# Node and attention rows gathered into the FFN by edge place, and a new order of its products on TensorE

## The reference, cut to what matters

```python
x = _layernorm(x + L0(x, rel_embed, norm, src, dst, rel_id, ...))     # x1
...
att = agg.reshape(n, NH * HD) @ Wo + bo        # agg is zero where the node has no incoming edge
x = residual + att                             # x2
h = _layer_norm(x, g2, b2)
ffn = gelu(h @ W1 + bf1, approximate=False) @ W2 + bf2
...
x = _layernorm(x1 + (x2 + ffn))
```

## Time and profile before

| | |
|---|---|
| median of 3 runs | 2438.21 us (2438.11 to 2440.93) |
| the profiled execution | 2436.44 us |
| its span, first to last instruction | 2434.7 us |
| mean granted TensorE clock | 0.962 |
| PE busy | 2066.7 us, 85% |
| DVE busy | 1912.1 us, 79% |
| ACT busy | 1330.5 us, 55% |
| POOL busy | 1228.3 us, 50% |
| DMA packets and volume | 353686, 413.33 MB |

### The profile page before, as it was taken

How to read it: one execution, slowest core, us unless ns; L and a number is a source line. 1 busy time by engine, 2 the same in 40 slices (tenths; PEclk the granted TensorE clock), 3 DMA queues, 4 the chain that set the end, 5 groups by cost and what they waited for, 6 DMA issues and landing times. The chain is left out here.

```text
span 2434.7 us, 49516 instructions
## 1 busy us (share of the span) xinstructions
PE 2066.7 (85%) x14383; PEld 1685.0 (69%) x14383; DVE 1912.1 (79%) x7786; ACT 1330.5 (55%) x3176; POOL 1228.3 (50%) x1418
## 2 busy tenths in 40 slices
PE   3777777759997888849999399992999999999998
PEld 2555555559997888737776289881777777777776
DVE  3999999978885889869997877773777777777774
ACT  1899999933332455568886200001556666566665
POOL 2764444247772777667772157775333333333332
PEclk9999999989998999979999699996999999999999
DMA  3888888779997688655552156664133333333321
GB/s 85 259 259 242 243 244 241 212 216 292 295 287 242 197 231 237 185 153 164 162 161 75 48 144 195 202 200 152 54 110 111 105 105 105 109 110 108 105 96 53
DMA packets 353686, 413.33 MB, mean 170 GB/s; under 512 B 51340, under 2 KB 235040, under 8 KB 353418
## 3 DMA queue, kind: packets, MB, share of 16 engines
q1 hardware_dynamic: 315850, 339.88, 44.3%
q0 software_dynamic: 34496, 69.37, 11.4%
q10 hardware_dynamic: 3072, 0.92, 0.2%
HBM read 263.50 MB, written 179.89 MB: 182 GB/s over the span
## 5 line engine op out<-in xcount | busy, mean ns | idle before, releaser
L1807 PEld LDWEIGHTS p_y<-w,g_T 128*128 128x128 f32 x3136 | 365.4, 192 | 46.4 <-issue 24.2
L1807 PE MATMUL p_y<-w,g_T 128*128 128x128 f32 x3136 | 365.8, 275 | 0.0
L1825 ACT ACTIVATE nT<-p_n 128x512 f32<-128x512 f32 x98 | 58.5, 597 | 560.3 <-PE p_n L1815 560.3
L1800 PE MATMUL p_f<-nT,w 128*128 128x512 f32 x784 | 354.0, 594 | 0.0
L1790 POOL TENSOR_TENSOR rstd<-var,minus_half 128x4 f32<-128x4 f32 x98 | 113.8, 1161 | 450.3 <-ACT res L1838 450.1
L547 POOL DMA_INDIRECT x_dst<-in_x_dram,idx x196 | 192.2, 981 | 226.9 <-DMA edge_x<-x_dst 144.3
L1832 ACT ACTIVATE g_T<-p_f,bf 128x512 f32<-128x512 f32 x392 | 266.7, 680 | 31.1 <-PE p_f L1800 31.0
L901 POOL DMA_INDIRECT h_src<-h_table,idx x196 | 189.5, 967 | 104.1 <-issue 58.6
L1800 PEld LDWEIGHTS p_f<-nT,w 128*128 128x128 f32 x784 | 141.9, 191 | 141.4 <-issue 141.4
L1597 POOL DMA_INDIRECT x_rows<-xv,idx x196 | 195.6, 998 | 77.8 <-issue 55.2
L1130 POOL DMA_INDIRECT x_src<-x_rows,idx x196 | 184.9, 943 | 85.4 <-issue 55.5
(11 more groups left out here) (321 smaller groups left out, 5548.6 us busy)
## 6 DMA issues: line engine op xcount, KB each, us to landing
xs<-x_rows SPq DMA_DIRECT2D x98, 512.0 KB, 3.7
x_in<-in_x_dram SPq DMA_DIRECT2D x98, 256.0 KB, 4.1
h_table<-h_rows SPq DMA_DIRECT2D x98, 256.0 KB
x_rows<-x_in SPq DMA_DIRECT2D x98, 256.0 KB, 2.9
out_dram<-res SPq DMA_DIRECT2D x98, 256.0 KB, 2.1
x_rows<-x_rows SPq DMA_DIRECT2D x50, 500.0 KB
edge_x<-x_dst SPq DMA_DIRECT2D x98, 128.0 KB, 2.6
h_own<-edge_x SPq DMA_DIRECT2D x49, 256.0 KB, 6.2
```

Source lines behind the costliest of these rows:

```text
L1800: e.matmul(p_f[ch][:], w_1[:, ch * P:(ch + 1) * P], nT[:, g % 2, :], start=True, stop=True).then_inc(f_prod, 1)
L1807: mm = e.matmul(p_y[g % 2][:, a * D:(a + 1) * D], g_T[:, g % 2, ch, a * P:(a + 1) * P], w_2[:, ch, :], start=(ch == 0), stop=(ch == FCH - 1))
```

## The change

**The tables.** `x_rows` keeps one row for each node and then one for each edge. `pair_rows` is new: for each of the 25088 edge places a pair, X1 and ATT (the attention output with bo added). `node_place` is new: for each node the edge place that holds its pair, or a number out of range (SKIP = 60000), with which the whole table is filled in `prepare`. POOL scatters the places, 4 B each: 49 scatters among dense's gathers, 147 in `weighted`.

```diff
-    x_rows = nc.dram_tensor("x_rows", [2 * N + EDGES, D], F32).ap()
-    both_table = x_rows[0:2 * N, :].rearrange("(n a) d -> n a d", a=2)
-    X1, X2 = range(2)
+    x_rows = nc.dram_tensor("x_rows", [N + EDGES, D], F32).ap()
+    pair_rows = nc.dram_tensor("pair_rows", [EDGES, 2, D], F32).ap()
+    X1, ATT = range(2)
+    node_place = nc.dram_tensor("node_place", [N, 1], I32).ap()
...
+        def scatter_place(e, t):
+            return e.indirect_dma_start(out=node_place, in_=edge_place[:, t:t + 1], in_offset=None,
+                                        out_offset=bass.IndirectOffsetOnAxis(ap=idx[:, AT_END, t:t + 1], axis=0),
+                                        bounds_check=N - 1, oob_is_err=False)
```

```diff
-                ON_ACT = 3
+                ON_ACT = 2
...
+                        if m % 2 and m // 2 < PLACED_EARLY:
+                            scatter_place(e, m // 2).then_inc(placed, 16)
...
-                            for a in range(GT):
-                                ins = e.bn_stats(stats[:, g % 2, a, :], x_in[:, g % XN, a, :])
+                            wait(e, shift_ready, g - 3)
+                            for r in range(GT // 2):
+                                ins = e.bn_stats(stats[:, g % 4, r, :, :].rearrange("p w k -> p (w k)"),
+                                                 x_in[:, g % XN, 2 * r:2 * r + 2, :].rearrange("p w d -> p d w"))
                             ins.then_inc(stats_ready, 1)
...
-                            for a in range(GT):
-                                ins = e.bn_aggr(mv[:, g % 4, a, :], stats[:, g % 2, a, :])
...
+                            e.wait_ge(shift_ready, g + 1)
                             for a in range(ON_ACT, GT):
                                 row = x_in[:, g % XN, a, :]
-                                ins = e.tensor_scalar(row, row, mv[:, g % 4, a, 0:1], rstd[:, g % 2, a:a + 1], ALU.subtract, ALU.mult)
+                                ins = e.tensor_scalar(row, row, rstd[:, g % 2, a:a + 1], shift[:, g % 2, a:a + 1], ALU.mult, ALU.add)
...
-                    chain(e.tensor_scalar(upper[:], src_col[:], -1.0, float(N), ALU.mult, ALU.add))
-                    chain(e.tensor_tensor(upper[:], base[:], upper[:], ALU.add))
-                    for at, twice in ((base, 1.0), (upper, 2.0)):
-                        chain(e.tensor_tensor(at[:], at[:], found[:], ALU.mult))
-                        chain(e.scalar_tensor_tensor(out=at[:], in0=src_col[:], scalar=twice, in1=at[:], op0=ALU.mult, op1=ALU.add))
+                    chain(e.tensor_tensor(base[:], base[:], found[:], ALU.mult))
+                    chain(e.tensor_tensor(base[:], base[:], src_col[:], ALU.add))
                     e.tensor_copy(idx[:, H_SRC, :], base[:])
-                    e.tensor_copy(idx[:, X_SRC, :], upper[:])
```

```diff
-                        if l == 0 and n < CHUNKS:
-                            e.dma_start(both_table[n * RUN:(n + 1) * RUN, X2, :], both_table[n * RUN:(n + 1) * RUN, X1, :]).then_inc(copied, 16)
...
+                    for q in range(7):
+                        part = slice(q * (EDGES // 7), (q + 1) * (EDGES // 7))
+                        e.dma_start(pair_rows[part, X1, :], x_rows[N:N + EDGES, :][part, :]).then_inc(pairs_in, 16)
...
                     for n in range(STEPS):
+                        if at_step(n, OUT):
+                            g = n - OUT
+                            e.wait_ge(row_ready, g + 1)
+                            e.dma_start(edges_of(pair_rows[:, ATT, :], g), att_out[:, g % ON, :].rearrange("p (j d) -> p j d", j=GT)).then_inc(stored[g % ON], 16)
...
+                    e.wait_ge(placed, 16 * T)
+                    for first in range(0, NG - 1, SLICE):
+                        last = min(first + SLICE, NG - 1)
+                        e.dma_start(place_in[:, first:last, :],
+                                    node_place[first * GROUP:last * GROUP, :].rearrange("(g p a) o -> p g (a o)", p=P, a=GT)).then_inc(places_in, 16)
+                    e.dma_start(place_in[:, NG - 1, :], node_place[N - GROUP:N, :].rearrange("(p a) o -> p (a o)", a=GT)).then_inc(places_in, 16)
+                    for k in range(ON):
+                        e.wait_ge(stored[k], 16 * len(range(k, GE, ON)))
+                    e.wait_ge(places_in, 16 * (len(range(0, NG - 1, SLICE)) + 1))
+                    e.wait_ge(pairs_in, 16 * 7)
...
-                    for g in range(GE):
-                        e.wait_ge(row_ready, g + 1)
-                        for j in range(GT):
-                            t = g * GT + j
-                            e.indirect_dma_start(out=both_table.rearrange("n a d -> n (a d)"),
-                                                 in_=xv[:, g % VN, j, :, :].rearrange("p a d -> p (a d)"), in_offset=None,
-                                                 out_offset=bass.IndirectOffsetOnAxis(ap=idx[:, AT_END, t:t + 1], axis=0),
-                                                 bounds_check=N - 1, oob_is_err=False).then_inc(scattered[g % VN], 16)
-                    for k in range(VN):
-                        e.wait_ge(scattered[k], scattered.after(k, GT * len(range(k, GE, VN))))
+                    for t in range(PLACED_EARLY, T):
+                        scatter_place(e, t).then_inc(placed, 16)
...
-                            e.wait_ge(own_ready, g + 1)
+                            e.wait_ge(weight_ready, g + 1)
                             wait(e, attT_ready, GT * (g - 1))
                             for j in range(GT):
                                 at = slice(j * P, (j + 1) * P)
-                                e.matmul(p_att[g % 2][:, at], w_src[:, g % 2, j, :], mate[:, g % 2, at], start=True, stop=False)
-                                mm = e.matmul(p_att[g % 2][:, at], w_own[:, g % 2, j, :], ident[:], start=False, stop=True)
+                                mm = e.matmul(p_att[g % 2][:, at], w_sum[:, g % 2, j, :], mate[:, g % 2, at], start=True, stop=True)
...
-                        if at_step(n, AHEAD + 2):
-                            g = n - AHEAD - 2
+                        if at_step(n, AHEAD + 3):
+                            g = n - AHEAD - 3
...
+                        e.wait_ge(out_prod, g + 1)
+                        wait(e, stored[g % ON], 16 * (g // ON))
+                        e.activation(att_out[:, g % ON, :], p_out[g % 2][:], ACT.Copy).then_inc(row_ready, 1)
```

```diff
-                            e.dma_start(xs[:, g % XN, :, :, :].rearrange("p a w d -> p (a w d)"),
-                                        rows(both_table, g).rearrange("(p a) w d -> p (a w d)", a=GT)).then_inc(xs_loaded[g % XN], 16)
+                            wait(e, pair_ready, g - XN + 1)
+                            e.dma_start(xs[:, g % XN, :, X1, :], rows(x_rows, g).rearrange("(p a) d -> p a d", a=GT)).then_inc(xs_in[g % XN], 16)
+                            e.dma_start(xs[:, g % XN, :, ATT, :], bo_rows[:].unsqueeze(1).to_broadcast([P, GT, D])).then_inc(xs_in[g % XN], 16)
...
+                            for a in range(GT):
+                                e.indirect_dma_start(out=xs[:, g % XN, a, :, :].rearrange("p w d -> p (w d)"), out_offset=None,
+                                                     in_=pair_rows.rearrange("n w d -> n (w d)"),
+                                                     in_offset=bass.IndirectOffsetOnAxis(ap=place_in[:, g, a:a + 1], axis=0),
+                                                     bounds_check=EDGES - 1, oob_is_err=False).then_inc(gathered[g % GN], 16)
...
+                            e.wait_ge(var_ready, m + 1)
+                            if m >= 4:
+                                wait(e, normed_ready, min(m - 3, NG))
+                                wait(e, res_ready, m - LATER - 3)
+                            e.tensor_tensor(rstd[:, m % 4, kinds, :], var[:, m % 2, kinds, :],
+                                            minus_half[:].rearrange("p (k a) -> p k a", k=2)[:, kinds, :], ALU.pow).then_inc(rstd_ready, 1)
...
-                        if at_step(n, A + 8):
-                            g = n - A - 8
-                            e.wait_ge(mv2_ready, g + 1)
-                            e.tensor_scalar(var2[:, g % 2, :], mv2[:, g % 4, :, 1], EPS, None, ALU.add).then_inc(var2_ready, 1)
-                            e.wait_ge(var2_ready, g + 1)
-                            wait(e, res_ready, g - 1)
-                            e.tensor_tensor(rstd2[:, g % 2, :], var2[:, g % 2, :], minus_half[:], ALU.pow).then_inc(rstd2_ready, 1)
...
-                        if at_step(n, A + 5):
-                            g = n - A - 5
+                        if at_step(n, A + 3):
+                            g = n - A - 3
                             e.wait_ge(nT_ready, g + 1)
...
-                        if at_step(n, A + 6):
-                            g = n - A - 6
+                        if at_step(n, A + 2):
+                            g = n - A - 2
```

(22 more changed lines are left out.)

369 lines of the change are left out of this document (180 added, 189 removed).

## The result

The changed kernel takes 2475.48 us (median of 4 runs, 2472.32 to 2476.42) against 2438.33 us for the kernel before (2438.11 to 2440.93): a ratio of 1.0148, 95% interval 1.013 to 1.0165. It is slower by 37 us. The profiled run has a span of 2473.5 us (2434.7 before, so +38.8) at a mean granted clock of 0.957. Forecast were 2447 us, slower, with a range of 2418 to 2480.

What follows compares the result with a forecast made beforehand. The prediction took PE to bound FFN, layer 0 and attention, and DVE with ACT dense. Terms led by FFN +89, weighted -62 and dense -16 summed to +8; with 1.8 for the median, 2447 us, range 2418 to 2480.

Steps and rivals of the forecast that it cites:

- FFN, steady: FFN's steps: p_y waits for its own group's gelus, period 8.35 us instead of 7.44, +89 us (60 to 104).
- lower bound of the forecast: FFN's steps: if res doesn't delay ACT, the last gelu ends at 4.32; +0.6 us a step, +60.
- POOL in FFN: FFN's steps: four gathers and one pow take POOL 6.3 to 7.4 us, hidden by one to two us.
- Rival C: FFN: POOL becomes the bound through a price at each change from gathers to pow; step 14.5 us, total 3050; chance 0.04.
- Rival D: FFN: PE's new gaps lower the clock to 0.95, some 40 us longer, 2487 us; chance 0.06.
- 49 of the scatters of places go into POOL's idle time: Dense: POOL, busy 215 of 461 us, has room for 49 scatters of 1.28 us, 63 us in all.
- DVE's share decides: Dense: DVE, ahead of ACT in busy time, saves 0.16 us a group; -16 us in all (-5 to -40).
- Layer 0: Layer 0: its 50 copies delay the first groups' loads, so only the start gains, -3.5 us.
- Weighted: Weighted, up to FFN's first load: PE's period falls from 4.98 to some 4.1 us; -62 us (-35 to -70).
- Rival B: Before FFN: node_place's loads in 16 B pieces cost up to 110 us instead of 12; 2470 to 2545; chance 0.06.
- FFN's start: FFN's start: load, fill and four gathers come before the first sum, normed one step sooner; +6 us (3 to 10).
- Layer 1: Layer 1: DVE loses its bn_aggr, but POOL and PE set the pace; -1 us.

Runs made afterwards that it cites:

- e3: Kernel before, with only FFN's order on PE changed: p_y follows p_f of the same group, p_n between them; 2528.17 us, ratio 1.0366.
- e1: Changed kernel, with FFN's p_y and the later sums, statistics and stores one group later again; 2399.79 us, ratio 0.9849.
- e2: Changed kernel, with ACT's four res of an FFN step behind its four gelus instead of between them; 2460.04 us, ratio 1.0085.
- e10: e1's kernel, with places 64 B apart in DRAM instead of 4 B, same early tiles; dense 424.1 us, total 2406.43 us in a single run.
- e7: e5's kernel, with three tiles normalised on ACT in dense and one on DVE; 2380.86 us, ratio 0.9763.
- e5: e1's kernel, with no place scatters in dense: 25 in softmax and 171 in weighted; 2395.99 us, ratio 0.9827.
- e9: Changed kernel, with three tiles normalised on ACT in dense instead of two; 2461.4 us, ratio 1.0092.
- e6: e1's kernel, with the last 49 tiles' places scattered early in dense instead of the first 49; 2383.24 us, ratio 0.9768.

## Why the prediction was right in its sign and short by 28 us

The sign and the size of the FFN term came out for the reason given. That 2475 still lies in the range, 4.5 us below its end, is in part luck: the end was set by a longer FFN step (+104), which did not occur, and the time got there by dense, weighted and layer 1, where nearly all misses went the same way.

**FFN, steady: right.** +89 forecast, +86.9 measured with the end. The period is 8.35 to the hundredth. The parts were 4.62 for the gelus (measured 4.62), 0.16 for wake-up and weight load, of which 0.06 lie ahead of p_y's start (4.68) and 0.10 behind it (p_y is 3.84 long, not 3.73), and 3.57. e3 shows the same in the kernel before, e1 the reverse, e2 the bound from below: a period of 8.05 without res between the gelus, which is what the lower bound of the forecast says (4.32 + 0.16 + 3.57). Whether to take that bound or the row was the choice, and the place of res in ACT's code decided it.

**POOL in FFN: right, by a hair.** Forecast 6.3 to 7.4 us a step, measured 4 x 1.3 and 2.04 with the gaps, 7.4: the upper end. It is hidden under 8.35 and only just under 7.44. Rival C (8 us at each change between gathers and arithmetic) did not occur: from the pow's end to the next gather pass 0.2 us. The rule of the Trainium skill (GPSIMD Engine Reference, 2.1 Instruction dispatch) on a freshly loaded kernel is borne out nowhere inside FFN's steps.

**The clock in FFN: right.** It is 1.00 over 800 us with a gap of 0.6 in each step. Rival D fell, and with it, here, the case in the Trainium skill (TensorE: Matmul & The Clock Gate, A second HAM failure mode). It fell to 0.91 in dense, between 200 and 250 us, where PE waited for up to 2.5 us at a time, behind ACT. In finer stretches, right behind the wait of 2.46 us that ends at 223.50 the granted clock is 0.53 from 225 to 230 us, the lower of its two levels (1.2 GHz) for nearly all of that time, and 1.00 again from 230 us.

**Dense: wrong, the largest miss.** The step that failed is "49 of the scatters of places go into POOL's idle time": they do, but I costed them by the engine that issues them and not by the DMAs that carry them. Without scatters DVE's savings give 422.6 to 424.3 instead of 433.9, so -10 to -11 instead of -16 (0.11 a group instead of 0.16). With the first tiles' scatters +9 to +21 come back (433.6 in the profiled run, 441.6 and 443.1 in two others), with the last tiles' scatters +2 to +4, with the first tiles' 64 B apart nothing (e10). "DVE's share decides" was right, and stronger than I used it: without scatters in dense the tile that the change moves from ACT to DVE costs 18 us of dense (406.3 in e7, 424.3 in e5) and 15 of the total, and I booked it as +0.23 a group without asking what dense would be without it. With the first tiles' scatters it costs 14 us of the total (e9), of which the profiled run shows 3.8 in dense.

**Layer 0: the mechanism right, the size short.** -5 forecast for its start and dense's end, -13.3 measured. I had the copies delay only the first loads; but from first to last p_acc the layer went from 240.7 to 233.3 as well, and PE from 97.75 to 100.00 of 100 us between 600 and 700. The loop takes 233.3 or 233.4 us in all ten kernels without the copies and 243.6 in e3, which has them. Between 600 and 700 us the DMA share falls from 0.97 to 0.71, and 17.8 us in which DVE waited for edge_rows are gone. So by the traces the 2% in which PE was not busy were transfers behind copies, though no run took the copies out alone, and the difference of 264 and 246.91 in the earlier trace rows held more than the start.

**Weighted: right mechanism, -51 instead of -62.** The steady step is 4.08 us, as forecast (4.1). What is missing is 7.4 us of waits for dstT and 9.1 for w_sum, both in the rows above: after each of DVE's divisions (a reciprocal of 1.55 and three products, every seven groups) w_sum comes late and a step takes some 6 us, 1.7 to 2.0 over the others. Before, the step after a division took 6.0 us as well, but against 4.98, so PE's longer step hid about half of that; I had read the 4.98 between two divisions. I had compared DVE's mean of 3.9 with 4.1 and put the upper bound at 4.3; it was 4.44. Some of it came back at the end: from the last p_att to FFN's first load pass 18.0 us, 22 to 23 were forecast. The loads of the places: 12 forecast, 10.7 measured from the first issue to FFN's first load. Rival B fell. That reading of the waits is from the trace alone; no run took the divisions out.

**FFN's start: +10.5 instead of +6.** Load and fill take 5.1 us to the first gather instead of 3.7, and the second group's gathers and the pow stand one behind the other on POOL, before the first normed.

**Layer 1: +5.8 instead of -1, open.** PE waited 32.5 us for gathered rows there instead of 22.4, though neither gathers nor their table changed in kind; in the ten kernels with the new tables the stretch from first to last p_acc was 245.0 to 249.5 us, against 243.8 before and 243.7 in e3. No run tells why.

Sum of the misses: dense +16, layer 0 -8, layer 1 +7, attention +3, weighted +11, FFN's start +4, the rest -1: +31 against the forecast of the span, 28 against the median.

## What to carry to other kernels

When a product on TensorE is moved to just behind the one whose output it needs, the price of each step is the latency of the engine between them less what fits into the gap; it can be read from one step of the timeline before anything runs, in the order in which that engine does its work. A transfer that is put into an idle engine's time is hidden only if the DMA engines have room as well: look at their share in the very stretch, at who waits there for a store, and at where the pieces land. And before work is moved between two engines that are both near their limit, ask what the stage would be with only the savings made; here the same change with one number left as it was is 14 us faster.

## What was not expected of the hardware

- 49 scatters of up to 128 pieces of 4 B, into a table with its entries 4 B apart in DRAM, raised the DMA share between 150 and 250 us of dense from 0.82-0.88 to 1.00-1.01, and ACT waited for stores of 256 KB for up to 3.1 us at a time (5.8 in e1). With the entries 64 B apart the share was 0.85 to 0.86 in the same 100 us and the longest such wait 0.8 us (e10); with targets farther down the table it was 0.89 to 0.93, and the longest wait 1.2 us from 100 us on, 3.4 before (e6). So the price of a scatter of small pieces is not only their number: how near to each other they land counts as well.
- A scatter on POOL takes 0.98 us, but up to 2.0 and 3.0 in softmax beside DRAM-to-DRAM copies and DVE's scans (e5). A pow over 128 x 8 takes 2.02 us (mean) in the changed kernel and 1.68 in e1, over 128 x 4 it takes 1.05 to 1.17.
- The same code of dense took 433.6, 441.6 and 443.1 us in one profiled run each of three kernels that differ only in FFN, and with the scatters spread apart it took 424.1. Here, where the DMA share is at 1.0, a single stage moves by 2% with no edit to it (whether from kernel to kernel or from run to run is not shown), and a difference of 10 us in the whole need not come from the edit.
